# Attention scores as three fp32r products, and GpSimd multiplying the scans by their rows of C

## What is computed

```
x = x + 0.5 * ffn0(ln(x))        # both operands rounded to an fp6 grid, 128x128 product
x = x + attn0(ln(x))             # one causal attention head
x = x + 0.5 * ffn0(ln(x))
x = x + 0.5 * heads(ln(x))       # 16 heads of width 64, gates choose 2 of 8 experts
x = x + mamba(ln(x))             # 256 channels, 16 states, scan over 512 tokens
x = x + 0.5 * heads(ln(x))
```

## Time and profile before

| | |
|---|---|
| median of 3 runs | 2796.3 us (2793.99 to 2802.63) |
| profiled execution, its own time | 2803.4 us |
| its span in the trace | 2801.5 us |
| mean granted TensorE clock | 0.966 of full speed |
| busy: PE, PEld | 2579.3 us (92%), 1712.1 us (61%) |
| busy: DVE | 2187.3 us (78%) |
| busy: ACT | 1855.6 us (66%) |
| busy: POOL | 737.2 us (26%) |

### The profile page before, as it was taken

The page is one execution under the profiler, slowest core; times in us unless marked ns, Lnnn a source line. Parts: engine busy times, 40 slices in busy tenths (PEclk is TensorE's granted clock), DMA queues, the critical chain, the costliest instruction groups (busy, mean ns, idle before and its releaser), DMA issues.

```text
span 2801.5 us, 51283 instructions
## 1 busy us (share of the span) xinstructions
PE 2579.3 (92%) x17437; PEld 1712.1 (61%) x17437; DVE 2187.3 (78%) x3233; ACT 1855.6 (66%) x4430; POOL 737.2 (26%) x564
## 2 busy tenths in 40 slices
PE   4499999998999998999899999999999999899997
PEld 2366665665666655666565665656566665666665
DVE  5688776889889788987987889797777878775552
ACT  2256665867678576875776867687677768666563
POOL 1000000345045214512540443064144315410000
PEclk8699999999999999999999999999999999999998
DMA  3234353564565646546464654666466465545434
GB/s 134 71 114 119 97 145 97 140 174 125 144 155 146 165 112 170 152 125 163 132 171 109 171 146 138 147 167 173 112 176 172 130 159 144 161 124 149 108 80 91
DMA packets 753407, 385.77 MB, mean 138 GB/s; under 512 B 421568, under 2 KB 678656, under 8 KB 752768
## 3 DMA queue, kind: packets, MB, share of 16 engines
q1 hardware_dynamic: 749216, 380.79, 51.4%
q10 hardware_dynamic: 3936, 1.70, 0.2%
HBM read 274.91 MB, written 115.87 MB: 139 GB/s over the span
## 4 chain that ended last, share of the span: by engine, by line
PE 59%; DVE 22%; issue 9%; ACT 3%; DMA 3%; POOL 2%; SPq 1%; DVEq 0%; ACTq 0%; POOLq 0%
PE ps L723 12%; PE ps L732 11%; PE ps L745 11%; PE ps L792 7%; DVE h_ring L1223 6%; PE ps L712 6%; PE ps L798 3%; DVE h_nmax L1043 3%; PE ps L805 2%; DVE h_ring L1233 2%; PE ps L764 1%; POOL h_ring L659 1%; PE ps L832 1%; ACT h_prob L891 1%; DVE h_wide_a L1195 1%
## 5 line engine op out<-in xcount | busy, mean ns | idle before, releaser
L891 ACT ACTIVATE h_prob<-ps,h_nmax 128x512 f32<-128x512 f32 x1024 | 710.6, 696 | 141.6 <-DVE h_nmax L1043 139.6
L1043 DVE TENSOR_REDUCE h_nmax<-ps 128x2 f32<-128x1024 f32 x512 | 621.9, 1215 | 142.7 <-PE ps L723 142.4
L732 PE MATMUL ps<-ident,h_prob 128*128 128x128 f32 x4096 | 623.6, 279 | 27.0 <-DVE h_probT L1283 15.2
L732 PEld LDWEIGHTS ps<-ident,h_prob 128*128 128x128 f32 x4096 | 481.2, 144 | 197.8 <-issue 120.9
L723 PE MATMUL ps<-h_qk 64*128 64x512 f32 x2048 | 587.6, 651 | 0.9 <-ACT h_prob L891 0.8
L668 POOL TENSOR_TENSOR h_wide_c<-h_wide_c,h_ring 128x512 f32<-128x512 f32 x240 | 331.1, 1380 | 731.7 <-DVE h_ring L1233 731.7
L1011 ACT ACTIVATE h_probT<-ps 128x512 f32<-128x512 f32 x796 | 478.7, 601 | 60.8 <-PE ps L732 57.9
L745 PE MATMUL ps<-h_probT,h_v_sb 128*64 128x256 f32 x4096 | 502.7, 388 | 5.8 <-DMA h_v_sb<-v_d 3.6
L745 PEld LDWEIGHTS ps<-h_probT,h_v_sb 128*64 128x64 f32 x4096 | 273.4, 137 | 314.5 <-issue 145.2
L1223 DVE TENSOR_TENSOR_SCAN h_ring<-h_ring 128x512 f32<-128x512 f32 x256 | 397.3, 1552 | 37.6 <-POOL h_ring L659 21.3
L659 POOL TENSOR_TENSOR h_ring<-h_m_xpad,h_m_b_rows 128x512 f32<-128x512 f32 x256 | 349.7, 1376 | 259.0 <-DVE h_m_xpad L1342 250.0
(11 more groups left out here) (222 smaller groups left out, 2678.5 us busy)
## 6 DMA issues: line engine op xcount, KB each, us to landing
h_mix_diag<-mix_blocks SPq DMA_DIRECT2D x128, 512.0 KB, 3.9
v_d<-h_v_mixed SPq DMA_DIRECT2D x128, 256.0 KB, 4.3
h_v_sb<-v_d SPq DMA_DIRECT2D x128, 256.0 KB, 3.4
at_d<-h_att SPq DMA_DIRECT2D x128, 256.0 KB, 2.8
h_mo_diag<-mo_blocks SPq DMA_DIRECT2D x128, 256.0 KB, 3.4
h_att<-at_d SPq DMA_DIRECT2D x128, 256.0 KB, 3.7
h_m_b_rows<-dbl_d SPq DMA_DIRECT2D x128, 256.0 KB, 4.3
h_m_c_rows<-dbl_d SPq DMA_DIRECT2D x128, 256.0 KB, 4.3
```

Source lines behind the costliest of these rows:

```text
L732: ins = pe.transpose(ps[:, TB + v % 2, k * P:(k + 1) * P], prob[:, v % NB, k * P:(k + 1) * P], ident[:, :])
L891: act.activation(prob[:, v % NB, :], ps[:, SB + v % 4, :], ACT.Exp, bias=nmax[:, p, j, o:o + 1], accum_out=den[:, p, j, o:o + 1]).then_inc ...
L1043: dve.tensor_reduce(nmax[:, p, j, :], ps[:, SB + 2 * w % 4:SB + 2 * w % 4 + 2, :], X, ALU.max, negate=True).then_inc(sem("row_max"), 1)
```

## The change

- `pq` and `pk` are copied out of PSUM twice by ACT: once rounded to fp32r (`qk_hi`), once in full (`qk_raw`, one buffer for both). GpSimd subtracts the one from the other into `qk_lo`, two steps after the piece's own step. ACT's second copy waits until GpSimd has taken the previous `qk_raw`. The scores become hi*hi + lo*hi + hi*lo, six fp32r matmuls of 64 rows instead of two fp32 ones, and wait for `qk_lo`.
- `pq` moves from step 8p-5 to 8p-9 and `pk` from 8p-4 to 8p-5.
- `read` moves from DVE to GpSimd, at the same step (scan's step + 1); `drive` moves one step earlier, `add` one step later.
- To make room, `x_prep`, `x_post`, `nrm` and `nT` become one buffer `x_io`; `chosen` has one copy instead of two; `g_rest` is written over `gates`. SP's load for "post" moves from step 14 to step 20 and waits until the next job's gates and the split of `nT` are done; the load for "prep" waits for the store of an earlier result. The `read` that is added below stands in GpSimd's program; the same function is removed from VectorE's.

```diff
-            + [(8 * p - 5, "pq", p) for p in range(PAIRS)] + [(8 * p - 4, "pk", p) for p in range(PAIRS)],
+            + [(8 * p - 9, "pq", p) for p in range(PAIRS)] + [(8 * p - 5, "pk", p) for p in range(PAIRS)],
...
+            x_io = t("x_io", [P, J, D])
+            ln["nrm"] = nrm = x_io
+            nT = x_io[:, :, :].rearrange("p j c -> p (j c)")
...
-            qk = t("qk", [P, 2, 2, S])
+            qk_hi = t("qk_hi", [P, 2, 2, S], F32R)
+            qk_lo = t("qk_lo", [P, 2, 2, S], F32R)
+            qk_raw = t("qk_raw", [P, S])
...
-                                if u == 14:
+                                if u == 20:
                                     if n >= 1:
                                         sp.wait_ge(sem("x_out"), 16 * n)
-                                    sp.dma_start(x_post[:, :, :], rows(x_in[n])).then_inc(sem("x_post_in"), 16)
+                                    if n + 2 < NJ:
+                                        wait_full(sp, "gate", 1, n + 2)
+                                        sp.wait_ge(sem("nT_split"), n + 3)
+                                    sp.dma_start(x_io[:, :, :], rows(x_in[n])).then_inc(sem("x_post_in"), 16)
...
+                    def read(b, v):
+                        n, h = divmod(v, HALVES)
+                        w = b * UN + v
+                        pool.wait_ge(sem(f"c_in{n % 2}"), 16 * (NS // 2 * b + n // 2 + 1))
+                        pool.wait_ge(sem("state"), w + 1)
+                        place = mb["scan"][:, w % NSC, :]
+                        pool.tensor_tensor(mb["y"][:, h, :] if n == 0 else place, place, mb["c_rows"][:, n % 2, :],
+                                          ALU.mult).then_inc(sem("read"), 1)
...
+                    def low_part(what, p, n):
+                        m = 0 if what == "pq" else 1
+                        wait_taken(pool, what, p, n)
+                        pool.tensor_tensor(qk_lo[:, p % 2, m, :], qk_raw[:, :],
+                                           qk_hi[:, p % 2, m, :].bitcast(F32), ALU.subtract).then_inc(sem("qk_lo"), 1)
...
-                                    if u == SCAN_AT[v] - 1:
+                                    if u == SCAN_AT[v] - 2:
                                         drive(n, v)
+                                for v in range(UN):
+                                    if u == SCAN_AT[v] + 1:
+                                        read(n, v)
                                 for v in range(HALVES, UN):
-                                    if u == SCAN_AT[v] + 1:
+                                    if u == SCAN_AT[v] + 2:
                                         add(n, v)
...
                         if j == 0:
-                            wait_taken(pe, "pk", p, i)
+                            pe.wait_ge(sem("qk_lo"), 2 * (PAIRS * i + p + 1))
                         if w >= 2:
                             pe.wait_ge(sem("prob"), 2 * w - 2)
-                        for o in range(2):
-                            ins = pe.matmul(ps[:, SB + 2 * w % 4 + o, :], qk[o * DH:(o + 1) * DH, p % 2, 0, j * P:(j + 1) * P],
-                                            qk[o * DH:(o + 1) * DH, p % 2, 1, :], start=True, stop=True)
+                        for k_, (q_, k) in enumerate(((qk_hi, qk_hi), (qk_lo, qk_hi), (qk_hi, qk_lo))):
+                            for o in range(2):
+                                ins = pe.matmul(ps[:, SB + 2 * w % 4 + o, :],
+                                                q_[o * DH:(o + 1) * DH, p % 2, 0, j * P:(j + 1) * P],
+                                                k[o * DH:(o + 1) * DH, p % 2, 1, :], start=(k_ == 0), stop=(k_ == 2))
...
-                            ins = act.activation(qk[:, c % 2, 0 if what == "pq" else 1, :], bank, ACT.Copy)
+                            act.activation(qk_hi[:, c % 2, 0 if what == "pq" else 1, :], bank, ACT.Copy)
+                            if PAIRS * n + c >= 1 or what == "pk":
+                                act.wait_ge(sem("qk_lo"), 2 * (PAIRS * n + c) + (what == "pk"))
+                            ins = act.activation(qk_raw[:, :], bank, ACT.Copy)
```

More of the change, by code:

```diff
@@ L278, in macaron_kernel @@
         for kind, n in BASE:
-            for u in range(-8, 110):
+            for u in range(-10, 110):
                 live_at.setdefault(step_of(kind, n, u), []).append((kind, n, u))
@@ L624, in _ @@
                                         sp.wait_ge(sem("x_mamba_out"), 16 * (b + 1))
-                                    if n >= 2:
-                                        sp.wait_ge(sem("normed"), n)
-                                    sp.dma_start(x_prep[:, :, :], rows(x_in[n])).then_inc(sem("x_prep_in"), 16)
+                                    if n >= 3:
+                                        sp.wait_ge(sem("x_out"), 16 * (n - 2))
+                                    else:
+                                        wait_full(sp, "gate", 1, n - 1)
+                                        sp.wait_ge(sem("nT_split"), n)
+                                    sp.dma_start(x_io[:, :, :], rows(x_in[n])).then_inc(sem("x_prep_in"), 16)
                                 for j in range(J):
@@ L705, in _ @@
                                     layer_norm_power(pool, "ln", ln, n)
+                            elif kind == "heads":
+                                for p in range(PAIRS):
+                                    for what in ("pq", "pk"):
+                                        if u == AT[what, p] + 2:
+                                            low_part(what, p, n)
                 @block.tensor
@@ L1094, in top2 @@
                         JH = J * H
-                        g = (gates[:, a] if r == 0 else g_rest)[:, :, :].rearrange("p j (h e) -> p (j h) e", e=E)
+                        g = gates[:, a, :, :].rearrange("p j (h e) -> p (j h) e", e=E)
                         top = g_top[:, :].rearrange("p (n a) -> p n a", a=1).broadcast_to([P, JH, E])
@@ L1120, in top2 @@
                             link(dve.scalar_tensor_tensor(
-                                out=g_rest[:, :, :].rearrange("p j c -> p (j c)"),
+                                out=gates[:, a, :, :].rearrange("p j c -> p (j c)"),
                                 in0=key.rearrange("p n e -> p (n e)"), scalar=NEG,
@@ L1300, in _ @@
                                 if u in NORM_AT:
-                                    layer_norm(dve, link, linked, x_prep if n else fbs[0]["x"], n, "ln", ln, NORM_AT.index(u), done=sem("normed"))
+                                    layer_norm(dve, link, linked, x_io if n else fbs[0]["x"], n, "ln", ln, NORM_AT.index(u), done=sem("normed"))
                                 if u == TOP_AT[0]:
@@ L1311, in _ @@
                             elif kind == "mamba":
-                                for v_ in range(UN):
-                                    if u == SCAN_AT[v_] + 1:
-                                        read(n, v_)
                                 if u == M_NORM_AT[0]:
```

40 lines of the change are left out of this document (12 added, 28 removed).

## The result

| | before | changed |
|---|---|---|
| median | 2797.23 us (4 runs, 2793.99 to 2802.63) | 2853.82 us (4 runs, 2850.66 to 2860.52) |
| span of the profiled execution | 2801.5 us | 2858.7 us |
| mean granted TensorE clock | 0.966 | 0.947 |

The ratio is 1.0204, with a 95% interval from 1.0177 to 1.023: the change made the kernel slower by 57 us. The prediction was 2747 us and faster; the measured time lies in its range and in the span of its slower rival (2839 to 2895).

What follows compares the result with a forecast made beforehand. PE was taken as the bound without scans, no engine as full with them; -32 (scores outside), -26 (scan stretches) and +8 (bank holding) made -50, so 2747 us against the runs' median, range 2680 to 2880.

Steps and rivals of the forecast that it cites:

- slower rival: Scan stretches: GpSimd becomes the bound, 5.9 to 6.1 us per scan, +43 to +99 us, 2839 to 2895; chance 0.29.
- The score step: PE's scores: six fp32r matmuls take 0.92 us on the chain instead of 1.06, a gain of 0.14 per step.
- The serial rival: PE's scores: the six fp32r matmuls run one after another, at least +216 us, above 3000; chance 0.07.
- Buffers, places and SP's moved waits: Shared x_io, moved steps and SP's load waits: no gain, priced at 0, up to +10 us kept for the range.
- ACT's second copies: 256 more ACT copies: hidden as work, but they hold PSUM banks longer; +8 us, bounds 0 and 49.
- The step that failed: Scan stretches: GpSimd fullest at 5.3 us per scan, plus 0.2 coupling, so 5.5 instead of 5.62; -26 us.
- longer blocked scans, 4.3 to 5.0: DVE in scan stretches: loses 0.73 us per scan, but blocked scans lengthen, leaving it 4.3 to 5.0 us.
- the signs that were to show the forecast wrong: DVE waiting over 100 us for the drive, copies waiting for low parts, score steps above 1.1, mean scans above 2, lower clock.
- The other term: Scores outside the scan stretches: 232 steps, each 0.14 us shorter on PE's chain, -32 us.

Runs made afterwards that it cites:

- e3: The kernel before with only the buffers shared (x_io, chosen, gates) and SP's load waits moved: 2799.51 us, ratio 1.0002.
- e5: The kernel before with only pq and pk moved, to steps 8p-9 and 8p-5: 2802.23 us, ratio 0.999.
- e6: e1 without ACT's second copy; GpSimd subtracts the rounded part from itself, so low parts are zero: 2819.69 us, ratio 1.0062 to the kernel before.
- e8: e1 with GpSimd subtracting only 64 of 512 columns for the low part, all else kept: 2759.81 us, ratio 0.986 to the kernel before.
- e1: The changed kernel with the read given back to VectorE, the new scores kept: 2827.68 us, ratio 1.0111 to the kernel before.
- e10: The kernel before with shared buffers, plus 256 GpSimd subtractions of 512 columns that nobody waits for: 2897.42 us, ratio 1.0325.
- e2: The kernel before with only the read moved to GpSimd, drive one step earlier and add one later: 2796.5 us, ratio 0.9999.
- e12: The kernel before with shared buffers and one fp32r product for the scores, no low parts: 2697.0 us, ratio 0.9615.
- e13: e12 with the read moved to GpSimd: 2690.76 us, ratio 0.9597 to the kernel before.

## Why the prediction was wrong

**What was right.** The score step was priced at 0.92 us on the chain; it is 0.89, with the two halves of the array side by side. The chain in order of time, 2560 to 2590 us (start, us, what), beside the earlier trace rows:

```profile
2561.36 0.92 PE ps L755 x6
...
2564.74 0.69 PE ps L743 x3
...
2565.87 0.89 PE ps L755 x6
```

The serial rival was wrong. Job 14 fell from the earlier trace rows's 144.5 us to 140.0, the 4.5 us that 32 score steps of 0.14 make:

```profile
L924 ACT ACTIVATE h_prob<-ps,h_nmax x64: 676/688/731, 2554.8 to 2694.8; 128x512 f32<-128x512 f32 x64
```

Buffers, places and SP's moved waits were priced at 0 and cost 0 (e3, e5). ACT's second copies were priced at +8; e6 doesn't contradict it, with 14 us for the copies and a shorter subtraction together.

**The step that failed** is the one from "GpSimd becomes the fullest, at 5.3" to "I add 0.2 for this coupling and take 5.5 us per scan", -26 for the scan stretches. Measured: 5.87 us per scan and +62. GpSimd's own load was not the trouble: it is busy 1247.28 us in 248 intervals, 5.03 us per scan, less than the 5.3. The coupling was: the interval is 0.84 us longer than GpSimd's work, where the sum had 0.2. The rows had a hint of this, since before the change the fullest engine, PE, had 5.24 us of work in an interval of 5.62.

The turns between the two engines were seen in the rows and worked out, but charged to GpSimd alone. I asked how much GpSimd time a scan needs, found that it fits, and let GpSimd's slack cover the rest. DVE's side was one clause ("longer blocked scans, 4.3 to 5.0") that didn't enter the sum, and it was limited to scans. They have 61 of the 244 us; DVE is busy 5.05 us per scan, just over the top of those bounds. DVE executes in order, and the row maximum, for which ACT and then PE wait, stands behind the operations that are held: this is the 139.6 us of ACT's idle time that became 220.9. Of the signs that were to show the forecast wrong, only the lower clock came. The one that was to show late GpSimd work, DVE waiting more than 100 us for the drive, stayed at 32.9, because the loss is inside busy times.

**The other term** that missed is -32 for the scores outside the scan stretches: the gaps came out at +4, the end at -8 and the part ahead of the scans at 0. Only the end gave what it should. e8 shows that the gain exists when the low part is small: there the stretches are -25, the gaps -7, the parts at both ends -10 each, together -52 of the span.

**The slower rival** had the right size (5.9 us per scan, +43 to +99) and the right resource, but its mechanism, a GpSimd that is full, is not what decides. In the scan stretches GpSimd is 65% busy in e1 and 61% in e10, and both are slower than the kernel before. Its 5.9 us were GpSimd's own work and turns, of which the trace has 5.03, so that the size agrees is luck. In the changed kernel GpSimd is also nearly full in the scan stretches (86%), and the read and the low part together cost 26 us more than the low part alone (1.0204 against 1.0111), where the read alone costs none; that this last part comes from fullness was not tested.

**Left open.** Why the 90 us that e2 takes off DVE bring nothing. 71 of them come back as idle time in which DVE waits for PE's scores, so DVE was not the one that came last there. Why PE's scores don't come earlier, no run shows. Open is also how the loss divides between DVE being held and PE's clock.

## What to carry to other kernels

An idle GpSimd is not free room. Before an elementwise operation that reads SBUF goes there, count the VectorE operations beside it that have two SBUF inputs, and charge their waiting to VectorE, in whose busy time it hides. A dummy operation that nobody waits for, once reading and once only filling, prices it in two runs. And when a gain of 0.17 us on one engine needs new work on others, price the version that does without that work first: here a single fp32r product, where its lower exactness will do, was worth 107 us, and three of them with their low parts cost 57.

## What was not expected of the hardware

Six fp32r matmuls of 64 rows and 512 columns in two halves of the array hold the chain for 0.89 us, against 1.06 for two fp32 ones; three of 128 rows for 0.69 to 0.70. GpSimd's operations are stretched by the turns as well: the read's median is 1.28 us and its longest 2.21 in the changed kernel.

With one product PE is busy 87% of the span instead of 92%, and the mean granted clock goes from 0.966 to 0.940 (e12) and 0.933 (e13): part of what PE saves is given back, since it works more often at the lower of its two levels.
